# A fifth exponential piece on VectorE: 1024 columns of channel 14, with a factored polynomial

## The reference, cut to what matters

```
Q, K, V = x @ Wq + bq, x @ Wk + bk, x @ Wv + bv       # split in 16 heads of 8
for each of 16 channels w:                            # cpm = cos(phase_modulators[w])
    scores = (Q * cpm[w]) @ (K * cpm[w]).T / sqrt(8)  # 512 x 512 for each batch and head
    scores = scores * cos(2.7e-12 * scores * scores)
    attn = softmax(scores)
    acc += (attn @ V) * interference_weights[w]
x = layernorm(x + (acc / 16) @ Wo + bo)
...                                                   # feed-forward with experts
x = layernorm(x + ffn(x))
```

## Time and profile before

| | |
|---|---|
| median of three runs | 3490.22 us (3489.55 to 3492.64) |
| the profiled execution, its own time | 3487.47 us |
| its span, first to last instruction | 3485.2 us |
| ScalarE busy | 3360.3 us (96%) |
| VectorE busy | 3068.6 us (88%) |
| TensorE busy, matmuls | 2674.0 us (77%) |
| GpSimd busy | 257.6 us (7%) |
| mean granted TensorE clock | 0.913 of full speed |

### The profile page before, as it was taken

The page is one execution under the profiler, slowest core; times in us unless marked ns, Lnnn a source line. Parts: engine busy times, 40 slices in busy tenths (PEclk is TensorE's granted clock), DMA queues, the critical chain, the costliest instruction groups (busy, mean ns, idle before and its releaser), DMA issues.

```text
span 3485.2 us, 47727 instructions
## 1 busy us (share of the span) xinstructions
PE 2674.0 (77%) x20599; PEld 766.9 (22%) x20599; DVE 3068.6 (88%) x2885; ACT 3360.3 (96%) x603; POOL 257.6 (7%) x325
## 2 busy tenths in 40 slices
PE   6777878778778778778777787877878778787773
PEld 2222222212222222222222222222222222222222
DVE  6888888888988898898889899989899999899867
ACT  6999999999999999999999999999999999999981
POOL 0000000000000000000010111110211110121111
PEclk7999999998999899999999999899899998999986
DMA  1000000000000000000000000000000000000001
GB/s 49 1 1 1 1 1 1 1 1 1 1 1 1 1 1 1 1 15 1 1 2 1 4 2 4 2 4 1 2 4 3 4 2 1 4 2 4 2 24 34
DMA packets 19174, 16.10 MB, mean 5 GB/s; under 512 B 4177, under 2 KB 16866, under 8 KB 18722
## 3 DMA queue, kind: packets, MB, share of 16 engines
q1 hardware_dynamic: 18130, 12.54, 1.2%
q10 hardware_dynamic: 720, 0.34, 0.0%
q0 software_dynamic: 128, 0.26, 0.0%
HBM read 7.76 MB, written 5.37 MB: 4 GB/s over the span
## 4 chain that ended last, share of the span: by engine, by line
issue 56%; ACT 32%; POOL 6%; ACTq 2%; DVE 2%; PE 1%; DMA 1%; SPq 0%; POOLq 0%; DVEq 0%
ACT probs L639 32%; ACTq L634 2%; POOL loop_memory L506 1%; POOL loop_memory L504 1%; POOL loop_memory L508 1%; POOL loop_memory L516 0%; POOL w_head L493 0%; ACTq L638 0%; POOL loop_memory L520 0%; ACT probs L656 0%; POOL loop_memory L550 0%; PE psum L1226 0%; DVE m_pad L796 0%; DVE probs L1123 0%; DVE probs L861 0%
## 5 line engine op out<-in xcount | busy, mean ns | idle before, releaser
L639 ACT ACTIVATE probs<-s_t 128x8192 f32<-128x8192 f32 x480 | 3324.0, 7021 | 1.6 <-issue 1.6
L1226 PE MATMUL psum<-probs,v_pad 128*27 128x512 f32 x15360 | 1980.1, 662 | 713.8 <-ACT probs L639 709.0
L1226 PEld LDWEIGHTS psum<-probs,v_pad 128*27 128x27 f32 x15360 | 476.5, 115 | 2117.2 <-issue 1073.0
L796 DVE TENSOR_REDUCE m_pad<-psum 128x4 f32<-128x2048 f32 x128 | 292.8, 2289 | 18.2 <-PE psum L759 16.9
L696 DVE SCALAR_TENSOR_TENSOR x_y<-s_t,c_last,x_2k 128x2048 f32<-128x2048 f32 x128 | 303.5, 2371 | 3.5
L809 DVE COPY s_t<-psum 128x2048 f32<-128x2048 f32 x126 | 287.9, 2285 | 18.5 <-PE psum L779 18.4
L704 DVE SCALAR_TENSOR_TENSOR x_p<-x_y 128x2048 f32<-128x2048 f32 x128 | 292.3, 2284 | 5.2 <-PE psum L728 4.9
L718 DVE SCALAR_TENSOR_TENSOR x_p<-x_p,x_2k 128x2048 f32<-128x2048 f32 x128 | 293.0, 2289 | 3.3
L714 DVE SCALAR_TENSOR_TENSOR x_p<-x_p,x_y 128x2048 f32<-128x2048 f32 x128 | 292.6, 2286 | 1.1
L710 DVE SCALAR_TENSOR_TENSOR x_p<-x_p 128x2048 f32<-128x2048 f32 x128 | 292.0, 2281 | 0.0
L1389 DVE RECIPROCAL r_z<-psum 128x48 f32<-128x48 f32 x192 | 80.5, 419 | 173.6 <-PE psum L1196 172.9
(11 more groups left out here) (235 smaller groups left out, 1136.8 us busy)
## 6 DMA issues: line engine op xcount, KB each, us to landing
x_next_dram<-x_p SPq DMA_DIRECT2D x1, 1024.0 KB, 3.8
x_group<-x_next_dram SPq DMA_DIRECT2D x1, 1024.0 KB, 4.9
loop_memory<-in_L_attn_x_dram SPq DMA_DIRECT2D x8, 128.0 KB, 2.1
x_dram<-loop_memory SPq DMA_DIRECT2D x8, 128.0 KB, 1.8
out_dram<-loop_memory SPq DMA_DIRECT2D x8, 128.0 KB, 1.8
x_dram<-probs SPq DMA_DIRECT2D x2, 512.0 KB, 3.9
out_dram<-probs SPq DMA_DIRECT2D x2, 512.0 KB, 3.6
s_t<-in_L_ffn_ew_dram SPq DMA_DIRECT2D x3, 256.0 KB
```

The lines of the kernel that those rows point to most:

```text
L639: nc.scalar.activation(probs[:, (p + w) % 2, :], s_t[:, p, :], ACT.Exp, scale=scales[(p + w) % 2]).then_inc(s["exp_done"], 1)
L796: nc.vector.tensor_reduce(m_pad[:, qt, :].rearrange("p (b l) -> p b l", l=L)[:, :, R_M:R_M + 1], banks(qt), AX.X, ALU.max, negate=True).th ...
L1226: last = nc.tensor.matmul(products_of(u, wg)[L * b:L * b + SLOTS * A, :], v_pad[:, p, b * T + kt, c0:c0 + SLOTS * A], probs[:, (p + w) % 2 ...
```

## The change

VectorE takes part of channel 14 too, and its polynomial is another one:

- At step 14 ScalarE computes only columns 0 to 7167 (ACT_LAST). The other 1024 columns (block kt = 3 of batches 2 and 3) are piece 4 on VectorE, with channel 14's scale. TensorE's matmuls of step 14 leave those two out, and the product of piece 4 adds them to the same bank, in two matmuls.
- A piece has seven ops instead of eight. The polynomial is now ((y + A) y + B) y = t, then (t + C) t + D, without its leading factor. The values come out multiplied by EXP2_ONE. For channel 15 that cancels in the division. For channel 14 ScalarE's part has to have the same factor: its exponential gets a bias, ln(EXP2_ONE), from a tile of one column, `ln_one`.
- There are 35 ops in a unit, and all hand-written tables are made anew. The bank of channels 12 to 14 is complete only after product 4, so channel 15 alone is copied and weighed before it (GROUP_AT).
- In the second half the small exponential L622 stands one step later on ScalarE, stage 5 three steps later and stage 5.5 two steps later on VectorE.

The diff, cut to its core:

```diff
+SHARED_B = 2
+ACT_LAST = T * X_COLS - (NB - SHARED_B) * S
-PIECES = T
+PIECES = T + 1
...
-PIECE_OPS = 8
+PIECE_OPS = 7
...
-PRODUCT_STEPS = {5: 0, 9: 1, 13: 2, WA + 1: 3}
+PRODUCT_STEPS = {5: 0, 7: 1, 10: 2, 14: 3, WA + 1: 4}
...
-GROUP_AT = [0, 1, 2, 3, 4, 5]
-LAST_GROUP_AT = [0, 1, 2, 3, 5, 4]
+GROUP_AT = [0, 1, 2, 3, 5, 4]
...
-FF_STEPS = {12: 1, 13: 2, 14: 2.5, 15: 3, 16: 4, 20: 5, 22: 5.5, 25: 5.7, 27: 6, 28: 7, 29: 7.5}
+FF_STEPS = {12: 1, 13: 2, 14: 2.5, 15: 3, 16: 4, 23: 5, 24: 5.5, 25: 5.7, 27: 6, 28: 7, 29: 7.5}
-FF_EXP_STEP = 18
+FF_EXP_STEP = 19
...
+                                if w == WA - 1:
+
+                                    nc.scalar.activation(probs[:, (p + w) % 2, 0:ACT_LAST], s_t[:, p, 0:ACT_LAST], ACT.Exp,
+                                                         bias=ln_one[:, 0:1], scale=scales[(p + w) % 2]).then_inc(s["exp_done"], 1)
+                                    continue
...
+            w, start, cols = (W - 1, n * X_COLS, X_COLS) if n < T else (WA - 1, ACT_LAST, T * X_COLS - ACT_LAST)
...
             if op == 4:
                 dve.wait_ge(s["piece_chain"], base + 3)
-                nc.vector.tensor_scalar(x_y[:], x_y[:], EXP2_V, None, ALU.add)
+                nc.vector.scalar_tensor_tensor(out=t, in0=t, scalar=EXP2_B, in1=y, op0=ALU.add, op1=ALU.mult) \
+                    .then_inc(s["piece_chain"], 1)
...
-            for b in range(NB):
-                last = nc.tensor.matmul(products_of(u, NWG - 1)[L * b:L * b + SLOTS * A, :],
-                                        v_pad[:, u % 2, b * T + n, VPAD:VPAD + SLOTS * A],
-                                        x_p[:, b * S:(b + 1) * S], start=(n == 0), stop=(n == PIECES - 1))
+            wg, kt = (NWG - 1, n) if n < T else (LAST_OF[WA - 1], T - 1)
+            c0 = VPAD if n < T else VPAD - A * SLOT_OF[WA - 1]
+            for b in range(NB) if n < T else range(SHARED_B, NB):
+                at = b * S if n < T else (b - SHARED_B) * S
+                last = nc.tensor.matmul(products_of(u, wg)[L * b:L * b + SLOTS * A, :],
+                                        v_pad[:, u % 2, b * T + kt, c0:c0 + SLOTS * A],
+                                        x_p[:, at:at + S], start=(n == 0), stop=(n == T - 1 or (n == T and u < UNITS - 1)))
...
-                            for b in range(NB):
+                            for b in range(SHARED_B if w == WA - 1 and kt == T - 1 else NB):
```

62 lines of the change are left out of this document (32 added, 30 removed).

## The result

The changed kernel takes 3467.34 us (median of 4 runs, 3465.88 to 3469.35), the kernel before 3489.9 in the same comparison (3489.55 to 3492.64). The ratio is 0.9935, 95% interval 0.9922 to 0.9947. The forecast was 3464.7 us with a range of 3460 to 3474. The profiled execution, the fastest of the four, took 3465.88 us with a span of 3463.6, 21.6 us less than the profiled one of before; forecast for it were 25.5 us less.

The account below looks back on a forecast made before the run. ScalarE, busy 96% of the span, was taken as the bound. -24.5 - 2.7 + 1 + 0.7 = -25.5 us against the profiled 3487.5 gave 3462.0, so 3464.7 us for the median, 8-in-10 range 3460 to 3474.

Parts of the forecast that it names:

- shorter exponential, less its bias: ScalarE, step 14: 1024 fewer columns save 0.857 us, the bias costs 0.091; 24.5 us less over 32 units.
- small exponential a step later: ScalarE, L622: both waits for VectorE's add, 0.21 us and 2.46 in the last unit, go; 2.7 us less.
- stalls behind TensorE: No stall in most units; 1 us over the whole run for matmuls at the low clock that start late.
- last unit: After the last products: one-channel weighing and last transposes come later, 1.1 us more, two fewer matmuls take back 0.4; +0.7 us.
- Rival 2: Step 14's exponential: the bias costs nothing on Exp; 3461.8 us, chance 0.1.
- The added work: VectorE: four pieces lose an op (4.91 us), the fifth costs 7.4; net 2.4 us more a unit, 1.8 to 2.8.
- rival 3: Second half, steps 4 to 7 and 12 to 0: VectorE becomes the bound, slower, 3513 us; chance 0.06.
- no step goes over 9.5 us: VectorE's lateness behind a step's exponential: step 5's reduction rises from 7.0 to 8.3 us, no step over 9.5.
- some 13 us: VectorE becoming the bound decides once a step's reduction or copy ends some 13 us after that step's exponential.
- The matmuls start 0.2 us late, 3.3 being allowed: Step 7, behind product 1 moved from step 9: matmuls start 0.2 us late, 3.3 us costing nothing.
- Rival 1: Products 1 and 2 make TensorE late where VectorE is fullest; ScalarE idles at steps 9 and 12; 3472 us, chance 0.17.
- rival 4: Step 14: step 13's products hold ScalarE at the low clock, at most 0.5 us a unit; 3481 us, chance 0.03.

Follow-up runs that it names:

- e5: Changed kernel with no bias operand on the exponential of step 14: 3458.88 us, ratio 0.9913 to the kernel before.
- e6: Changed kernel with step 14's exponential full again (8192 columns, bias kept), VectorE still doing the fifth piece: 3496.44 us, ratio 1.0018 to the kernel before.
- e11: Kernel before with one edit, the small exponential at step 19 instead of 18: 3485.95 us, ratio 0.9991 to the kernel before.
- e4: Changed kernel with the small exponential back at step 18 instead of 19: 3480.62 us, ratio 0.9972 to the kernel before.
- e10: Changed kernel with later products, GpSimd's last additions held back, no bias, and a fifth piece of 1536 columns instead of 1024: 3454.86 us, ratio 0.9897.
- e1: Changed kernel with product 1 at step 8 instead of 7 and product 2 at 11 instead of 10: 3460.51 us, ratio 0.9916 to the kernel before.
- e2: Changed kernel with the fifth piece computed on 64 columns instead of 1024, its product still reading 1024: 3474.37 us, ratio 0.9956 to the kernel before.
- e3: Changed kernel without the fifth piece, all exponentials 8192 columns, the seven-op polynomial and its steps kept: 3493.02 us, ratio 1.0006 to the kernel before.

## Why the prediction was right, and where its terms were off

The bound, the price of columns and the bias held. The forecast for the profiled execution was 3462.0 us and it took 3465.9; at the median the distance is 2.6 us and not 3.9, because the changed kernel's profiled execution lies 1.5 us below its median and not 2.7, as that of before did. That last microsecond is luck. Term by term, for the two profiled executions:

| term | forecast us | measured us | from |
|---|---|---|---|
| shorter exponential, less its bias | -24.5 | -24.6 | 32 x (103.84 - 103.07); e5, e6 |
| small exponential a step later | -2.7 | -3.7 to -4.4 | first to last exponential, less the other terms; e11 |
| stalls behind TensorE | +1 | +4.7 | idle time of L646 |
| last unit | +0.7 | +2.0 | last exponential to comb |
| sum | -25.5 | -21.6 | |

- **Shorter exponential.** Right to 0.1 us, and e6 gives it back whole (27.1 us with the bias kept; its units are 103.93 us against 103.84 before, the bias again). Rival 2, a bias that costs nothing, fell with e5.
- **Small exponential.** Mis-sized low: I summed the two waits that I had on the timeline, where the group in the earlier trace rows has 3.4 us, and e11 finds 4.4. Beside the change's other parts it is worth far more, 13.3 us (e4), which the prediction didn't see: it priced the step against VectorE as it stood before.
- **VectorE.** The added work was 2.56 us a unit for 2.4, and it was hidden: rival 3's wait ahead of the reciprocal shrank. Of its lateness the prediction said no step goes over 9.5 us. That holds for the first half at the median (the reductions end 8.3 to 9.2 us behind their exponential, 8.7 at step 5 where 8.3 were counted); in the second half it is 9.1 to 10.8 us at the median and up to 12.9. e10 shows that the limit which it gave for rival 3, some 13 us, is about right: with 12.2 to 14.2 us behind at the median, stalls come, in five of sixteen units.
- **Stalls: the step that was mis-sized.** "The matmuls start 0.2 us late, 3.3 being allowed" came from one unit at the high clock. At the median product 1 ends 1.0 us behind its exponential and not 0.2 (0.5 in the first half, 1.3 in the second), which costs nothing. What costs is a unit in which it is up to 3.4 us behind: because the products of step 4 ran at the low clock and VectorE waited 3 us for their transposes, or, in the second half, because of VectorE's own work. Product 1, two steps earlier than before, has no room for either. TensorE then idles some 3 us, and behind that its clock falls. I priced late starts and the low clock as if they met by chance, 1 us for both together; they aren't independent, since the low clock followed all 31 waits of 3 us and more. e1 moves the products and the stalls go; e2 and e6 leave them and the stalls stay, e2's at step 12. Rival 1 had the mechanism and its places (steps 9 and 12), with 8 us at the median where the profiled run shows 4.7 and the gain of e1 6.8.
- **Last unit.** The weighing came later as said, by 0.7 to 1.0 us in eight other profiles. That step 13's matmuls at the low clock end behind a shortened exponential is rival 4's mechanism, met once there and once at 256.04 (0.39 us), not in every unit. Steps as slow as rival 4 needs (over 6 us) number twelve in the trace of before, not eleven, and twelve in the changed kernel.

What stays open: why a step now and then runs at the low clock behind the idle time that it always has; why the long waits for a piece recur every 4 or 8 units in some kernels (e3, e6), and not at all in e5; and what made the medians of e1 and e2 differ from the changed kernel's by 3 us more than the profiled executions do.
